# Row maxima of an attention layer taken one or two at a time, in a kernel whose order of stages is written out by hand

## The reference, cut to what matters

```python
q, k, v = (qkv[0], qkv[1], qkv[2])
attn = jnp.einsum('bhnd,bhmd->bhnm', q, k) * scale
attn = jax.nn.softmax(attn, axis=-1)
out = jnp.einsum('bhnm,bhmd->bhnd', attn, v)
```

## Time and profile before

| what | value |
|---|---|
| time, median of 3 runs | 4647.7 us (4629.57 to 4753.43) |
| the profiled execution's own time | 4622.95 us |
| its span, first to last instruction | 4621.2 us |
| TensorE matmuls busy | 4023.6 us, 87% |
| TensorE weight loads busy | 3167.6 us, 69% |
| VectorE busy | 2592.3 us, 56% |
| ScalarE busy | 1759.5 us, 38% |
| GpSimd busy | 375.3 us, 8% |
| mean granted TensorE clock | 0.875 of full speed |
| chain that ended last | PE 74%, DVE 13%, ACT 5% |

### The profile page before, as it was taken

The page is one execution under the profiler, slowest core; times in us unless marked ns, Lnnn a source line. Parts: engine busy times, 40 slices in busy tenths (PEclk is TensorE's granted clock), DMA queues, the critical chain, the costliest instruction groups (busy, mean ns, idle before and its releaser), DMA issues.

```text
span 4621.2 us, 70067 instructions
## 1 busy us (share of the span) xinstructions
PE 4023.6 (87%) x27744; PEld 3167.6 (69%) x27744; DVE 2592.3 (56%) x7217; ACT 1759.5 (38%) x2774; POOL 375.3 (8%) x523
## 2 busy tenths in 40 slices
PE   2789898998898889888989889899889888988888
PEld 1557677776777777677777677777677777767666
DVE  3445655556665556656555666555665555665433
ACT  1234333344333344334434433344433334433332
POOL 2000000000000000000000000000000000000000
PEclk7668888888899898889989889988889989888889
DMA  4201111111111101111101111111111110111000
GB/s 118 42 18 35 33 27 38 24 30 38 34 27 38 30 26 35 34 31 34 38 19 35 38 34 27 38 28 26 38 34 27 38 31 25 35 27 17 14 14 4
DMA packets 153944, 147.06 MB, mean 32 GB/s; under 512 B 64347, under 2 KB 131924, under 8 KB 153620
## 3 DMA queue, kind: packets, MB, share of 16 engines
q1 hardware_dynamic: 147192, 139.67, 14.0%
q10 hardware_dynamic: 6428, 2.91, 0.3%
HBM read 87.21 MB, written 7.91 MB: 21 GB/s over the span
## 4 chain that ended last, share of the span: by engine, by line
PE 74%; DVE 13%; ACT 5%; issue 2%; SPq 2%; DMA 2%; POOL 1%; ACTq 0%; POOLq 0%; DVEq 0%
PE area_a L1048 16%; PE area_n L1056 13%; PE area_b L1048 11%; PE area_m L1056 8%; PE area_n L1275 4%; PE area_n L1080 3%; DVE mx L952 2%; ACT pT_both L676 2%; PE area_m L1225 2%; PE area_a L1131 2%; PE area_b L1071 2%; SPq L464 2%; DVE scratch L963 1%; PE area_b L1206 1%; PE area_a L1206 1%
## 5 line engine op out<-in xcount | busy, mean ns | idle before, releaser
L952 DVE TENSOR_REDUCE mx<-area_n 91x1 f32<-91x273 f32 x1152 | 473.1, 432 | 171.3 <-PE area_n L1275 155.8
L1056 PE MATMUL area_n<-w_dn,hid 128*91 128x192 f32 x2304 | 500.4, 383 | 46.5 <-DVE mrow L957 38.7
L1056 PEld LDWEIGHTS area_n<-w_dn,hid 128*91 128x91 f32 x2304 | 430.1, 192 | 96.8 <-issue 59.8
L1048 PE MATMUL area_a<-xT,w_gu 96*128 96x273 f32 x1536 | 424.3, 421 | 57.5 <-DVE y L915 38.2
L1275 PE MATMUL area_n<-k1s,q1s 96*91 96x273 bf16 x1152 | 329.5, 338 | 117.8 <-DVE mx L952 93.1
L1048 PE MATMUL area_b<-xT,w_gu 96*128 96x273 f32 x1536 | 408.5, 410 | 0.0
L1048 PEld LDWEIGHTS area_a<-xT,w_gu 96*128 96x128 f32 x1536 | 299.9, 204 | 146.1 <-DVE y L915 48.0
L1048 PEld LDWEIGHTS area_b<-xT,w_gu 96*128 96x128 f32 x1536 | 294.4, 196 | 65.5 <-ACT scratch L644 3.1
L1275 PEld LDWEIGHTS area_n<-k1s,q1s 96*91 96x91 bf16 x1152 | 137.7, 135 | 266.8 <-DVE mx L952 196.5
L621 ACT ACTIVATE pa<-area_a,scal 91x820 bf16<-91x820 f32 x192 | 180.2, 939 | 291.7 <-PE area_a L1131 268.4
L963 DVE RECIPROCAL scratch<-area_n 128x273 f32<-128x273 f32 x96 | 179.1, 1866 | 159.7 <-PE area_n L1296 159.7
(11 more groups left out here) (242 smaller groups left out, 7434.9 us busy)
## 6 DMA issues: line engine op xcount, KB each, us to landing
img<-in_x SPq DMA_DIRECT2D x192, 392.0 KB, 3.4
q1s<-scratch SPq DMA_DIRECT2D x192, 102.4 KB, 3.5
k1s<-scratch SPq DMA_DIRECT2D x192, 102.4 KB, 4.4
out<-outb SPq DMA_DIRECT2D x32, 204.8 KB
q0s<-scratch SPq DMA_DIRECT2D x128, 25.6 KB, 3.4
k0s<-scratch SPq DMA_DIRECT2D x128, 25.6 KB, 2.6
pooled<-pooled_dram SPq DMA_DIRECT2D x128, 9.2 KB
tokens<-in_txt SPq DMA_DIRECT2D x32, 57.8 KB
```

The source lines that it names most:

```text
L952: v.tensor_reduce(mx[:, k:k + 1], N[0:TC, k % 2, 0:T], AX.X, ALU.max)\
L1048: last = mm(area[x][0:rows_, j, 0:n], w(j, kc), rhs[:, kc, 0:n], start=(kc == 0), stop=(kc == NK - 1))
L1056: last = mm(by_token(x)[:, c, :], lhs(i, c), w_, start=(i == 0), stop=(i == len(w) - 1))
```

## The change

The stage mx is now a pair: there are 18, mx.0 to mx.17. Stage mx.k does the maxima 2k and 2k + 1 of before: two matmuls, one in each bank of area N, with one full signal behind the second, then one reduction of 91 x 2 x 273 scores into two columns of `mx`, with one taken signal. TensorE waits with `begin` in place of `begin_bank`. In TURN each pair stands at the place where the first of its two maxima stood; the place of the second falls away. All other stages keep their order, and offsets, areas, DMAs and the arithmetic stay as they are.

```diff
 TURN = """
-tok n4s n4n n4f cw n0s n1s n2n n0n qk1.0 qk1.1 v2 n0f qk0.0 pool.0 qk0.1 n2f ey.0 v1 ez.0 ey.1 mx.0 mx.1 mx.2 n1n gate
-mx.3 ez.1 mx.4 pool.1 k1 mx.5 v0 a0.0 mx.6 mx.7 ey.2 cl.0 cl.1 ez.2 mx.8 r3 mx.9 mx.10 rta a0.1 cl.2 dy.0 cl.3 pk0
-a0.2 mx.11 mx.12 mx.13 mx.14 mx.15 pk1 ey.3 ez.3 mx.16 r2 mx.17 gt mx.18 vs mx.19 pv.0 mx.20 og.0 mx.21 s1.0 mx.22
-mx.23 s1.1 mx.24 ey.4 ez.4 ey.5 mx.25 ez.5 t1.0 mx.26 mx.27 t1.1 mx.28 rtb mx.29 cl.4 mx.30 cl.5 a0.3 c1 mx.31 mx.32
-mx.33 mx.34 mx.35 ct pool.2 mt dy.1 a2.0 pool.3 wo a2.1 a2.2 a2.3 a2.4 cl.6 a2.5 cl.7 pw.0 os.0 a2.6 pool.4 pv.1 og.1
+tok n4s n4n n4f cw n0s n1s n2n n0n qk1.0 qk1.1 v2 n0f qk0.0 pool.0 qk0.1 n2f ey.0 v1 ez.0 ey.1 mx.0 mx.1 n1n gate ez.1
+mx.2 pool.1 k1 v0 a0.0 mx.3 ey.2 cl.0 cl.1 ez.2 mx.4 r3 mx.5 rta a0.1 cl.2 dy.0 cl.3 pk0 a0.2 mx.6 mx.7 pk1 ey.3 ez.3
+mx.8 r2 gt mx.9 vs pv.0 mx.10 og.0 s1.0 mx.11 s1.1 mx.12 ey.4 ez.4 ey.5 ez.5 t1.0 mx.13 t1.1 mx.14 rtb cl.4 mx.15 cl.5
+a0.3 c1 mx.16 mx.17 ct pool.2 mt dy.1 a2.0 pool.3 wo a2.1 a2.2 a2.3 a2.4 cl.6 a2.5 cl.7 pw.0 os.0 a2.6 pool.4 pv.1
...
                     elif name == "mx":
                         t.await_full("N", stage)
-                        v.tensor_reduce(mx[:, k:k + 1], N[0:TC, k % 2, 0:T], AX.X, ALU.max)\
+                        v.tensor_reduce(mx[:, 2 * k:2 * k + 2], N[0:TC, :, 0:T], AX.X, ALU.max)\
                             .then_inc(taken["N"], 1)
...
                     elif name == "mx":
                         if k == 0:
                             pe.wait_ge(stack_in, n * STACK_DMAS + STACK_DMAS)
-                        t.begin_bank("N", stage, "mx")
-
-                        hh, c = divmod(k, NC_)
-                        mm(N[0:TC, k % 2, 0:T], q1s[0:SROWS, hh, c * TC:(c + 1) * TC], k1s[0:SROWS, hh, :],
-                           start=True, stop=True).then_inc(full["N"], 1)
+                        t.begin("N", stage)
+
+                        for i in range(2):
+                            hh, c = divmod(2 * k + i, NC_)
+                            last = mm(N[0:TC, i, 0:T], q1s[0:SROWS, hh, c * TC:(c + 1) * TC], k1s[0:SROWS, hh, :],
+                                      start=True, stop=True)
+                        last.then_inc(full["N"], 1)
```

More of the change, by code:

```diff
@@ L51 @@
 TURN = """
-tok n4s n4n n4f cw n0s n1s n2n n0n qk1.0 qk1.1 v2 n0f qk0.0 pool.0 qk0.1 n2f ey.0 v1 ez.0 ey.1 mx.0 mx.1 mx.2 n1n gate
-mx.3 ez.1 mx.4 pool.1 k1 mx.5 v0 a0.0 mx.6 mx.7 ey.2 cl.0 cl.1 ez.2 mx.8 r3 mx.9 mx.10 rta a0.1 cl.2 dy.0 cl.3 pk0
-a0.2 mx.11 mx.12 mx.13 mx.14 mx.15 pk1 ey.3 ez.3 mx.16 r2 mx.17 gt mx.18 vs mx.19 pv.0 mx.20 og.0 mx.21 s1.0 mx.22
-mx.23 s1.1 mx.24 ey.4 ez.4 ey.5 mx.25 ez.5 t1.0 mx.26 mx.27 t1.1 mx.28 rtb mx.29 cl.4 mx.30 cl.5 a0.3 c1 mx.31 mx.32
-mx.33 mx.34 mx.35 ct pool.2 mt dy.1 a2.0 pool.3 wo a2.1 a2.2 a2.3 a2.4 cl.6 a2.5 cl.7 pw.0 os.0 a2.6 pool.4 pv.1 og.1
-a2.7 ob.0 a2.8 a2.9 pw.1 os.1 a2.10 a2.11 ob.1 mg n3s n3n ey.6 ey.7 pool.5 ez.6 pw.2 os.2 ey.8 ez.7 ez.8 n3f a0.4 cl.8
-cl.9 dy.2 f0.0 f0.1 ob.2 f0.2 ey.9 ez.9 pr1 n5s a0.5 n5n cl.10 cl.11 fd ey.10 pv.2 ey.11 og.2 ez.10 n5f ez.11 pr0 dy.3
-rtr
+tok n4s n4n n4f cw n0s n1s n2n n0n qk1.0 qk1.1 v2 n0f qk0.0 pool.0 qk0.1 n2f ey.0 v1 ez.0 ey.1 mx.0 mx.1 n1n gate ez.1
+mx.2 pool.1 k1 v0 a0.0 mx.3 ey.2 cl.0 cl.1 ez.2 mx.4 r3 mx.5 rta a0.1 cl.2 dy.0 cl.3 pk0 a0.2 mx.6 mx.7 pk1 ey.3 ez.3
+mx.8 r2 gt mx.9 vs pv.0 mx.10 og.0 s1.0 mx.11 s1.1 mx.12 ey.4 ez.4 ey.5 ez.5 t1.0 mx.13 t1.1 mx.14 rtb cl.4 mx.15 cl.5
+a0.3 c1 mx.16 mx.17 ct pool.2 mt dy.1 a2.0 pool.3 wo a2.1 a2.2 a2.3 a2.4 cl.6 a2.5 cl.7 pw.0 os.0 a2.6 pool.4 pv.1
+og.1 a2.7 ob.0 a2.8 a2.9 pw.1 os.1 a2.10 a2.11 ob.1 mg n3s n3n ey.6 ey.7 pool.5 ez.6 pw.2 os.2 ey.8 ez.7 ez.8 n3f a0.4
+cl.8 cl.9 dy.2 f0.0 f0.1 ob.2 f0.2 ey.9 ez.9 pr1 n5s a0.5 n5n cl.10 cl.11 fd ey.10 pv.2 ey.11 og.2 ez.10 n5f ez.11 pr0
+dy.3 rtr
 """.split()
```

## The result

The changed kernel takes 4794.67 us (median of three runs, 4794.03 to 4799.08) against 4647.7 for the kernel before: 147 us more. It is slower, in the direction that was forecast, and by 147 us where 67 were forecast. The profiled execution took 4799.08 us (span 4797.1) at a mean granted clock of 0.846, where the one of before took 4622.95 at 0.875. So the two profiles stand 176 us apart.

The account below looks back on a forecast made before the run. TensorE's order of work was taken as the bound. To the profiled 4623 us came 51 us of direct waiting (1.65 per turn) and 4 for the last turn, giving 4678, then 36 for the clock: 4714, rounded to 4715; range 4640 to 4800.

Parts of the forecast that it names:

- The walk at unchanged clock: One turn followed from mx.0 to mt with the clock as before: mt 1.65 us later, 51 us over 31 turns.
- the gate: Behind pairs 0 and 1 back to back: its matmuls start 1.55 us after the first maximum instead of 1.00.
- wait of pair 5: Before rta: pair 5 waits 1.3 to 1.4 us for pair 4, where mx.10 waited 1.07.
- pv.0 against gt: Around vs, now queued behind the whole pair 9: pv.0 is released by vsum and later against gt by 0.7 us.
- rounds: Where a pair stands directly behind a pair: 1.25 us from one start to the next.
- mx.31's place to mt: End of the stretch: two pairs at this place's slower clock take 3.0 us, leaving mt 1.65 later.
- idle time before the matmuls: TensorE's idle time before the matmuls of mx, whole run: 160 to 190 us instead of 117.8.
- the second term: The clock: half instead of a quarter of the turns become irregular, 1.15 us per turn more, 36 us.
- Rival (c): The clock falls in every turn, first stretch near 52 us: 4779, or 4840 with all turns as the longest; chance 0.28.
- Rival (a): VectorE bounds the stretches of maxima, so fewer, longer reductions shorten them: 4605 us, at the extreme 4505; chance 0.06.
- Rival (d): All pairs are covered by other work and the time does not move: 4623 to 4650 us; chance 0.07.
- (b): The direct cost of the pairs holds but the clock is unchanged: 4678 us; chance 0.19.

Follow-up runs that it names:

- the filled kernel: The changed kernel with dummy matmuls, results used by nothing, before the waits of five pairs (1, 5, 7, 14, 17): 4689.39 us.
- The places alone: The kernel before with its 36 single maxima and one-bank lead kept, moved two by two to where the pairs stand: 4739.87 us, ratio 1.028.
- the version with moved singles: The kernel before with three of its 36 single maxima moved from places with a wait to places with room: 4582.81 us, ratio 0.993.

## Why the prediction was right and wrong

The direction, the bound and the place were right. TensorE's order of work sets the time, the loss is in the stretch from mx.0 to mt, and the 90 us behind it kept their length.

The walk at unchanged clock held at the places that were looked up. Pair 1 starts 1.21 us after the first maximum and the gate 1.48 (1.55 was said); wait of pair 5, 1.36 (1.3 to 1.4); pv.0 against gt 0.94 later (0.7); rounds of 1.22 to 1.25 between pairs (1.25); mx.31's place to mt 3.00 us (3.0); pair reduction 720 ns (0.73); idle time before the matmuls 166.4 us (160 to 190). Its sum of 1.65 us per turn, 51 us, stands against 1.9 us more idle time per turn, and against 2.1 by the filled kernel at equal clock, 65 us.

The step that failed is the second term, "I take half instead of a quarter, an estimate: 1.15 us per turn more, 36 us". By the same comparison it measured 3.8 us per turn, 118 us (4.0 by the busy time), even above the bound set beside it (3.4, 105 us). Every turn became a long one; the bound was low because it took the mean of the irregular turns, 141, and not the 143.3 of the longest, though those stood in the earlier trace rows. Rival (c), with 0.28, is what happened: it said 4779, or 4840 if all turns were as the longest. The 4840 is summed wrongly: it leaves out the direct 51 us and counts the eight long turns twice. At 143.3 us for each of 31 turns, 5.5 above the mean of before, 4623 + 170 = 4793 comes out, close to what was measured, although no direct cost is in it. Its point of decision, a clock of the stretch under 0.80, was the right thing to look at (0.75 now).

What was wrong in the reasoning is to treat the clock as a risk spread over turns, and to tie it to added waiting. The places alone, with 0.5 us more idle time per turn, made the same matmuls 3.4 us slower per turn. The turns of a steady loop follow one another alike: 22 of 29 here, 27 of 29 in the version with moved singles. The regular turn of before was such a state, and even 0.75 us of pure waiting broke it, at three times its own cost or more. The half that I took had no row behind it.

Rival (a), fewer and shorter reductions as a gain, is refuted where it could be seen alone: VectorE's 44 us less bought nothing, and the same pairs at roomy places (4650) reach the kernel before and no more. Its 117.8 us "of waits, all behind single reductions" was a misreading too: 93.1 us of them stood behind VectorE and 20.9 behind the DMAs of k. Rival (d) fell with 166.4 us of idle time, and (b), the direct cost alone, is what the filled kernel shows: 4689 against the 4678 said.

Shown, then, is that two thirds of the loss are the same matmuls at a lower grant, and that an empty wait or another order of the same work is enough to bring it down. What stays open is which activity ahead of a stretch decides its clock. Dummies ahead of pair 1 raised it, dummies ahead of n4f did not, and moving work with hardly any wait added lowered it. Why the turns prefer 136.5, 139.9, 143.3 and 146.8 us is seen and not explained by these runs.

## What to carry to other kernels

Merging two small steps that pass through both banks of a buffer takes the lead away from the engine that fills it: before merging, look for other work between any two (a full round was 1.25 us here, and places with 0.8 us or more were enough to win 145 us back), and move the steps if there is none. In a loop bound by TensorE, a fraction of a microsecond of waiting per turn can cost more than itself, here two to three times, because it can change which stretches are granted the full clock; price a change by TensorE's idle and its busy time apart, and look at turn lengths in a row to see what the loop has settled on. A wide spread of runs is itself a finding: here the slower a run of before, the lower its mean granted clock (0.883 at 4582.69 us, 0.852 at 4744.38), the one trace of it mixes short and long turns, and a version that keeps to the short kind is faster in the median without a shorter best turn.

## What the runs showed of the hardware that was not expected

- 0.75 us of idle time per turn, 23 us in all, cost 73 us; 1.5 us cost 94; in the changed kernel the same 0.75 us cost 49.
- 0.8 us of idle time filled with useless matmuls once per turn gained 36 us; five such places gained 105 us, with 22 more matmuls per turn.
- The same 867 or so matmuls of a turn are busy 122.4 us in a turn of clock 0.90 and 127.2 to 128.7 in one of 0.86.
- The same matmuls in another order, with 16 us more idle time over 29 turns, were busy 97 us longer.
- Single reductions in a row start 0.35 to 0.42 us apart though each shows 0.43, so two cost 0.78; one over both banks costs 0.72. Halving the instructions gained an eighth of their time (473.1 to 414.6 us).
